# Two MLPs, attention between them: when weights are split, and in which order the seam to the last MLP runs

## The chip, the cores and the metric

The kernel runs on one core of a Trainium2 chip. The core has five engines with their own instruction queues: TensorE (PE, matrix products into PSUM), VectorE (DVE), ScalarE (ACT), GpSimd (POOL) and SyncE (SP, which here only issues DMAs). They meet only in semaphores: an engine adds to one when an instruction ends, another waits for a value. The metric is the device time of one launch in microseconds (us). The kernel before takes 1842.34 us, the median of three runs (1841.61 to 1843.49).

## The reference

Two layers on 1024 tokens (4 sequences of 256) of width 512, each stage ending in a normalized residual. What matters here:

```python
# layer 0: a state-space mixer (projection, convolution, scan, output projection), then an MLP on int weights
h = silu(x @ gate_w.T * gate_s) * (x @ up_w.T * up_s)     # 1376 hidden columns, padded to 11 tiles of 128
y = (h @ down_w.T) * down_s
# layer 1: attention, 32 query heads in 8 groups, rotary embedding, causal softmax, output projection Wo
# then an MLP whose weights are made from pairs (w, base):
d = w - base; weight = base + mean(abs(d)) * sign(d)      # w1, w3: 1792 hidden columns (14 tiles); w2: down
h = silu(x @ w1.T) * (x @ w3.T); out = h @ w2.T
```

Everything is float32. Matrix products are made in a faster form (fp32r) on pairs of operands: each operand is split into a high part (a rounded copy) and a low part (operand minus high part), and a product is the sum of high x high, high x low and low x high.

## The kernel before

The program is a row of phases, each a block in which every engine has its own list of instructions; at the end of a phase the engines meet at a barrier. In order: load, `n0` (first normalization), `in` (projection), `par`, `scan`, `fa` (output projection), `mi` (first MLP's widening), `fb` (first MLP's down projection), `kv` (keys and values), the attention phase with the last MLP's widening inside it, and `fd` (last down projection, results stored). `fa`, `fb` and `fd` are one function, `finish_phase`.

**finish_phase** goes over 8 tiles of 128 tokens. For tile t ScalarE copies the hidden tile to its high part `hh` (L253), GpSimd subtracts to get the low part `hl` (L300), TensorE does 3K products of 128x512 (L235 to L237; K is 11 in `fb`, 14 in `fd`), and VectorE, GpSimd and ScalarE normalize and add. Before the first tile the down weights themselves are split: ScalarE copies K rows to `wh` (L284), VectorE subtracts K rows to `wl` (L426), and TensorE's first tile waits for row k of both, and for `hh` and `hl`.

**widen_phase** (`mi`) goes over 11 tiles f of the hidden width: ScalarE makes the high part of weights f+1 (L523), VectorE the low part (L591), TensorE does 48 products (L503), ScalarE applies silu (L552), VectorE multiplies (L618). Beside it, in the first 8 steps, GpSimd subtracts (L579) and ScalarE sums absolutes (L528) of the last MLP's weight pairs, to find their mean difference. At its end SP loads the first MLP's down weights (`ahead`).

**The attention phase** goes over 8 groups g and 4 batches b. At batch b TensorE does the queries of the next batch (L1355), the output projection of the batch before (L1380 to L1382), the transposes and value products of this batch (L1389 to L1402), and the scores of the next one (L1366, L1368). The queries of the next batch are rotated before their scores: ScalarE turns them, GpSimd multiplies by the sine (L1631), VectorE by the cosine (L1703), and VectorE adds the two (`rotate`, L1710), which raises `q_done`. At b = 2 of groups 0 to 6, GpSimd subtracts the low part of the next group's query weights right behind the sine (`query_weights`, L1635), 2048 columns. At b = 0 it does the same for output weights (L1639).

**The seam** to the last MLP starts in the last group. Normalizations of attention's result (`y_moments_of`, `y_scale`, `y_shift`, `y_norm`), the residual (`residual`, GpSimd, L1647), normalizations for the MLP (`x_moments_of`, `x_scale`, `x_shift`, `x_norm`), transposes of tokens (L1412), their split (`token_high` L1530, `token_low` L1771), and the making of the first two weight tiles (`difference` GpSimd L1655, `difference_sign` ScalarE L1534, `whole` and `whole_down` VectorE L1778 and L1787, `mlp_high` ScalarE L1541, `mlp_low` GpSimd L1659) stand in each engine's list in an order written by hand. TensorE does hidden tiles 0 and 1 by halves of the tokens (`widen_batch`, parts of 24 products at L1418) as tokens come ready, and from tile 2 whole tiles of 48 products of 128x512. SP loads the next weight pair when both the low parts and the down row of two tiles before are made.

Of the kernel before, what the change touches and what calls it, by code (L numbers as in the profile page):

```python
# [159 lines left out]
def finish_phase(nc, tag, M, place, K, hidden=None, gate=None, w_raw=None, acc=None,  # L160
                 out_scale=None, last_out=None, norm_only=False, ahead=(), x_loads=()):
# [9 lines left out]
    gated, h_hi, h_lo = sem("hidden_gated"), sem("hidden_hi"), sem("hidden_lo")  # L171
    y_ready, scaled = sem("y_ready"), sem("y_scaled")
# [7 lines left out]
    if proj:  # L180
        wh = place("wh", [P, K, DM], F32R)
        wl = place("wl", [P, K, DM], F32R)
# [19 lines left out]
    with nc.Block() as block:  # L202
# [15 lines left out]
        def _(pe):  # L218
# [7 lines left out]
            def step(t, s):  # L226
                if proj and t < TT:
# [3 lines left out]
                    for k in range(K):  # L231
# [3 lines left out]
                        nc.tensor.matmul(ps_y[s], hh[s][:, k, :], wh[:, k, :], start=(k == 0), stop=False)  # L235
                        nc.tensor.matmul(ps_y[s], hh[s][:, k, :], wl[:, k, :], start=False, stop=False)  # L236
                        mm = nc.tensor.matmul(ps_y[s], hl[s][:, k, :], wh[:, k, :], start=False, stop=(k == K - 1))  # L237
# [8 lines left out]
        def _(act):  # L246
# [34 lines left out]
            if proj:  # L281
                hidden_hi(0, 0)
                for k in range(K):
                    nc.scalar.activation(wh[:, k, :], w_raw[:, k, :], ACT.Copy).then_inc(split_w, 1)  # L284
# [4 lines left out]
        def _(pool):  # L289
# [39 lines left out]
        def _(dve):  # L329
# [93 lines left out]
            if proj:  # L423
                for k in range(K):
                    dve.wait_ge(split_w, k + 1)
                    nc.vector.tensor_tensor(wl[:, k, :], w_raw[:, k, :], f32(wh[:, k, :]), ALU.subtract).then_inc(split_wl, 1)  # L426
# [8 lines left out]
def widen_phase(nc, tag, M, place, F, kind, raw_dram, base_dram=None, hidden=None,  # L435
                x_conv=None, gate=None, scales=None, coeff=None, second=None, diff=None, raw=None, base=None, ahead=()):
# [12 lines left out]
    tap = sem("tap")  # L449
    d_in, d_sub, d_abs = [sem("diff_in0"), sem("diff_in1")], sem("diff_sub"), sem("diff_abs")  # L450
# [7 lines left out]
    if diff is not None:  # L458
        DC = DIFF_COLS // N_SUMS
        dw = [place(f"dw{i}", [P, 3, DC]) for i in range(2)]  # L460
        dm = [place(f"dm{i}", [P, 3, DC]) for i in range(2)]
# [6 lines left out]
    with nc.Block() as block:  # L468
# [43 lines left out]
        def _(act):  # L512
# [17 lines left out]

            def step(f, s):
                if exists(f + 1, F):
                    prepare(f + 1, 1 - s)
                if diff is not None and exists(f, N_SUMS):
                    differences(f, s)
                if kind == "ssm":
# [51 lines left out]
        def _(dve):  # L588
# [12 lines left out]
            def step(f, s):  # L601
                if kind == "int" and exists(f + 1, F):
                    int_lows(f + 1, 1 - s)
                if kind == "diff" and exists(f + 1, F):
# [20 lines left out]
            paired_steps(dve, F, step)  # L625
            if kind != "ssm":
                dve.wait_ge(second_done, F)
# [1451 lines left out]
```

## Time and profile before

| | |
|---|---|
| median of 3 runs | 1842.34 us (1841.61 to 1843.49) |
| the profiled execution: its time, its span | 1840.51 us, 1838.7 us |
| PE busy | 1676.4 us (91%) |
| PEld, DVE | 1376.5 us (75%), 1097.3 us (60%) |
| ACT, POOL | 869.0 us (47%), 822.2 us (45%) |
| mean granted clock of TensorE | 0.971 |

The profile is of one execution. Busy time is the time in which an engine ran an instruction; PEld is TensorE's weight load beside its products. Rows of the timeline give the start, the duration, the engine, the line and the operands of one or more instructions; in brackets the idle time before them and what ended it. The granted clock (PEclk) is a share of TensorE's full speed, 1.0 being 2.4 GHz and 0.5 being 1.2 GHz.

### The profile page before, as it was taken

To read this page: it belongs to the slowest core of one execution; us is meant where nothing else is said; L and a number is where in the kernel's file an instruction comes from. 1 tells how busy PE (TensorE), PEld (TensorE's weight loads), DVE (VectorE), ACT (ScalarE), POOL (GpSimd) and SP (SyncE) were. 2 spreads that over 40 slices of the span, in tenths; PEclk is the share of its full clock that TensorE was granted. 3 is DMA by queue.
4 is the path that set the end of the run, shared out by engine and by line. 5 is a ranking of instruction groups with operands and counts; after the bars stand their busy time and mean duration, and the time that the engine had idled before them with its cause. 6 is when DMAs were issued, how large, how long until landed. Compare 5 with 4: busy or idle time off the path is not lost. (4 is left out here: it accounts for less than half of the span.)

```text
span 1838.7 us, 24233 instructions
## 1 busy us (share of the span) xinstructions
PE 1676.4 (91%) x8214; PEld 1376.5 (75%) x8214; DVE 1097.3 (60%) x1592; ACT 869.0 (47%) x1761; POOL 822.2 (45%) x416
## 2 busy tenths in 40 slices
PE   5994999999998799898989999999999998799988
PEld 4851788888886688676877778787788786778777
DVE  4326999999995332452915666666666767622232
ACT  2336777777763353333624445454444545433231
POOL 2200999999984362342512232222222323365353
PEclk9997999999999899998999999999999999999989
DMA  3101100011100394001100010000100010144100
GB/s 113 63 1 72 47 35 35 36 34 35 34 0 24 134 355 163 18 1 57 63 23 24 24 47 23 23 23 23 46 23 23 23 58 35 70 142 160 42 18 29
DMA packets 25188, 100.84 MB, mean 55 GB/s; under 512 B 3104, under 2 KB 3360, under 8 KB 22560
## 3 DMA queue, kind: packets, MB, share of 16 engines
q1 hardware_dynamic: 24976, 99.89, 15.1%
q8 instruction: 40, 0.66, 0.1%
q14 instruction: 28, 0.23, 0.0%
q10 hardware_dynamic: 144, 0.07, 0.0%
HBM read 97.72 MB, written 2.23 MB: 54 GB/s over the span
## 5 line engine op out<-in xcount | busy, mean ns | idle before, releaser
L1001 PE MATMUL psum<-scratch_s,res_const 128*128 128x256 f32 x1024 | 250.4, 383 | 4.7 <-DVE scratch_s L960 4.0
L1631 POOL TENSOR_TENSOR stretch_turned<-stretch_turned,res_const 128x1024 f32<-128x1024 f32 x32 | 80.3, 2509 | 386.6 <-ACT stretch_turned L1492 386.6
L1001 PEld LDWEIGHTS psum<-scratch_s,res_const 128*128 128x128 f32 x1024 | 191.8, 190 | 43.0 <-DVE scratch_s L960 18.3
L858 POOL TENSOR_TENSOR scratch_s<-scratch_s,scan_cm 128x1024 f32<-128x1024 f32 x64 | 150.9, 2358 | 27.6 <-DVE scratch_s L944 27.6
L944 DVE TENSOR_TENSOR_SCAN scratch_s<-psum,scratch_s 128x512 f32<-128x512 f32 x128 | 153.4, 1198 | 8.5 <-ACT psum L899 8.5
L1355 PE MATMUL psum<-opnd_xh,query_wqh 128*128 128x256 f32 x512 | 151.5, 296 | 1.9 <-PEq L94 1.9
L846 POOL TENSOR_TENSOR scratch_s<-scan_bm,scratch_s 128x1024 f32<-128x1024 f32 x64 | 150.9, 2359 | 0.1
L1355 PE MATMUL psum<-opnd_xh,query_wql 128*128 128x256 f32 x512 | 145.6, 284 | 0.0
L1355 PE MATMUL psum<-opnd_xl,query_wqh 128*128 128x256 f32 x512 | 145.5, 284 | 0.0
L1500 ACT ACTIVATE stretch_pa<-psum,stretch_nm 128x128 f32<-128x128 f32 x128 | 45.2, 365 | 197.0 <-DVE stretch_nm L1722 197.0
L995 PE MATMUL psum<-scan_diag,scratch_s 128*128 128x256 f32 x512 | 132.9, 383 | 0.5 <-ACT scratch_s L891 0.5
L899 ACT ACTIVATE psum<-ssm_dt,ssm_vec 128x255 f32 (+1 forms) x256 | 110.8, 465 | 11.8 <-DVE scratch_s L944 11.3
L995 PEld LDWEIGHTS psum<-scan_diag,scratch_s 128*128 128x128 f32 x512 | 95.9, 193 | 13.0 <-ACT scratch_s L891 0.9
L1355 PEld LDWEIGHTS psum<-opnd_xh,query_wqh 128*128 128x128 f32 x512 | 99.0, 193 | 3.2 <-issue 2.3
L1380 PE MATMUL psum<-stretch_woh,stretch_oh 128*128 128x512 f32 x256 | 100.3, 392 | 0.5 <-DVE stretch_ol L1823 0.5
L1381 PE MATMUL psum<-stretch_wol,stretch_oh 128*128 128x512 f32 x256 | 100.0, 390 | 0.0
L1382 PE MATMUL psum<-stretch_woh,stretch_ol 128*128 128x512 f32 x256 | 99.9, 390 | 0.0
L1355 PEld LDWEIGHTS psum<-opnd_xl,query_wqh 128*128 128x128 f32 x512 | 98.9, 193 | 0.8
L1355 PEld LDWEIGHTS psum<-opnd_xh,query_wql 128*128 128x128 f32 x512 | 98.7, 193 | 0.0
L235 PE MATMUL psum<-stretch_wh,stretch_hh 128*128 128x512 f32 x176 | 71.1, 404 | 17.2 <-ACT stretch_wh L284 15.5
L960 DVE TENSOR_TENSOR scratch_s<-psum,scan_cm 128x512 f32<-128x512 f32 x128 | 85.2, 665 | 0.0
L950 DVE TENSOR_TENSOR_SCAN psum<-scan_decay,psum 128x512 f32<-128x512 f32 x64 | 78.1, 1221 | 0.0
(269 smaller groups left out, 4322.4 us busy)
## 6 DMA issues: line engine op xcount, KB each, us to landing
mi_dw<-in_dw SPq DMA_DIRECT2D x24, 448.0 KB, 5.7
mi_dm<-in_dm SPq DMA_DIRECT2D x24, 448.0 KB, 6.4
query_raw<-in_w_q SPq DMA_DIRECT2D x8, 1024.0 KB, 4.7
query_raw<-in_w_o SPq DMA_DIRECT2D x8, 1024.0 KB, 4.8
scan_cm<-bc_rows SPq DMA_DIRECT2D x12, 512.0 KB, 4.1
gu_raw<-in_w_gu SPq DMA_DIRECT2D x11, 512.0 KB, 8.0
mlpa_raw<-in_w_mlp SPq DMA_DIRECT2D x7, 768.0 KB, 4.3
mlpa_base<-in_b_mlp SPq DMA_DIRECT2D x7, 768.0 KB, 5.8
```

Source lines behind the costliest of these rows:

```text
L846: nc.gpsimd.tensor_tensor(by_state(shared[r][h]), bm[:, 4 * h:4 * h + 4, :], u[r].rearrange("p (a t) -> p a t", a=1).broadcast_to((P, 4, S ...
L858: nc.gpsimd.tensor_tensor(shared[r][h], shared[r][h], weights(4 * h, 4), ALU.mult).then_inc(weighted_pool, 1)
L899: ins = nc.scalar.activation(by_state(bank)[:, n, 1:SEQ], flat_dt[:, bass.ds(s * SEQ + 1, SEQ - 1)], ACT.Exp, scale=M.vec[:, bass.ds(s * N ...
L944: nc.vector.tensor_tensor_scan(quarter(r, i), decay_shared[i % 2], quarter(r, i), 0.0, ALU.mult, ALU.add).then_inc(scanned, 1)
L960: nc.vector.tensor_tensor(own[i], state[i], weights(NH + 2 * i, 2), ALU.mult).then_inc(weighted, 1)
L995: mm = nc.tensor.matmul(by_state(state[i])[:, :, t * P:(t + 1) * P], ut[r][:, t * P:(t + 1) * P], diag[:, t, 2 * i:2 * i + 2, :], start=Tr ...
L1001: mm = nc.tensor.matmul(ps_y[r], ident, part[:, n * SEQ:(n + 1) * SEQ], start=False, stop=stop and (n + 1) * SEQ == part.shape[1])
L1355: mm = nc.tensor.matmul(ps_q[:, h * SEQ:(h + 1) * SEQ], w[:, k, h * HD:(h + 1) * HD], x[:, k, b * SEQ:(b + 1) * SEQ], start=(k == 0 and w ...
L1380: nc.tensor.matmul(X[t], oh[:, t, part], woh[:, h, :], start=(h == 0), stop=False)
L1381: nc.tensor.matmul(X[t], oh[:, t, part], wol[:, h, :], start=False, stop=False)
L1382: mm = nc.tensor.matmul(X[t], ol[:, t, part], woh[:, h, :], start=False, stop=(h == HPG - 1))
L1631: nc.gpsimd.tensor_tensor(heads(turned[:, :]), heads(turned[:, :]), over_heads(C_SIN, SEQ), ALU.mult).then_inc(q_sine, 1)
```

## The change

1. `query_weights` on GpSimd (b = 2, groups 0 to 6) waits for `q_done` of the batch whose sine it has just made. In the last group `difference(1)` moves behind the same wait, `residual(0)`, `residual(1)` and `mlp_low(0)`.
2. The hand-written order of the seam changes on all four engines.
3. The down weights of the last MLP are split in its widening: ScalarE and VectorE do row f-1 at step f. Those of the first MLP are split in steps 7 to 10 of `mi`; they are loaded in phase `fa` now. Low parts are made in place.
4. `finish_phase` with ready halves (`fb`, `fd`) begins otherwise: `hh` of the first tile in two parts, TensorE does all products with `wh`, then with `wl`, then waits for `hl`, which VectorE makes, and not GpSimd.
5. Places of tiles in SBUF change to suit.

```diff
@@ finish_phase, TensorE
+                if proj and t == 0 and halves is not None:
+                    pe.wait_ge(h_first, 1)
+                    for k in range(K):
+                        if k == K // 2:
+                            pe.wait_ge(h_hi, 1)
+                        nc.tensor.matmul(ps_y[s], hh[s][:, k, :], wh[k], start=(k == 0), stop=False)
+                    for k in range(K):
+                        nc.tensor.matmul(ps_y[s], hh[s][:, k, :], wl[k], start=False, stop=False)
+                    pe.wait_ge(h_lo, 1)
+                    for k in range(K):
+                        mm = nc.tensor.matmul(ps_y[s], hl[s][:, k, :], wh[k], start=False, stop=(k == K - 1))
+                    mm.then_inc(y_ready, 1)
@@ finish_phase, ScalarE
+            if proj and halves is not None:
+                nc.scalar.activation(hh[0][:, 0:K // 2, :], hidden(0, 0)[:, 0:K // 2, :], ACT.Copy).then_inc(h_first, 1)
+                nc.scalar.activation(hh[0][:, K // 2:K, :], hidden(0, 0)[:, K // 2:K, :], ACT.Copy).then_inc(h_hi, 1)
@@ finish_phase, GpSimd
-                hidden_low(0, 0)
+                if halves is None:
+                    hidden_low(0, 0)
+                else:
+                    pool.wait_ge(h_lo, 1)
@@ finish_phase, VectorE
+            if proj and halves is not None:
+                dve.wait_ge(h_hi, 1)
+                nc.vector.tensor_tensor(hl[0][:, :, :], hidden(0, 0), f32(hh[0][:, :, :]), ALU.subtract).then_inc(h_lo, 1)
@@ widen_phase: rows_at = {f: range((f - 7) * F // 4, (f - 6) * F // 4) for f in range(7, F)}
+                for k in rows_at[f]:                       # ScalarE, before the silu of step f
+                    nc.scalar.activation(next_wh[:, k, :], next_raw[:, k, :], ACT.Copy).then_inc(next_hi, 1)
+                    for k in rows_at[f]:                   # VectorE, before the product of step f
+                        dve.wait_ge(next_hi, k + 1)
+                        nc.vector.tensor_tensor(next_wl[:, k, :], next_raw[:, k, :], f32(next_wh[:, k, :]), ALU.subtract).then_inc(next_lo, 1)
@@ attention phase, last MLP
+    def down_rows(f):
+        return {2: (0,), 3: (1,), 4: (2, 3), F1 - 1: (F1 - 2, F1 - 1)}.get(f, (f - 1,))
...
+                nc.scalar.activation(down_halves[0][k], down[:, k, :], ACT.Copy).then_inc(down_hi, 1)
...
+                nc.vector.tensor_tensor(down_halves[1][k], down[:, k, :], f32(down_halves[0][k]), ALU.subtract).then_inc(down_lo, 1)
@@ TensorE
             weights_split(0)
             pe.wait_ge(exped, U)
             widen_batch(0, 0)
+            token_transposes(2)
+            token_transposes(3)
             weights_split(1)
             widen_batch(1, 0)
-            token_transposes(2)
-            token_transposes(3)
-            widen_batch(0, 1)
             token_transposes(4)
             token_transposes(5)
+            widen_batch(0, 1)
             widen_batch(1, 1)
             pe.wait_ge(added, 2 * U)
             widen_batch(2, 2)
             token_transposes(6)
+            token_transposes(7)
             pe.wait_ge(half_kept, 1)
             widen_batch(3, 2)
-            token_transposes(7)
@@ GpSimd, body
                 if b == 2 and not (isinstance(g, int) and g == GROUPS - 1):
+                    pool.wait_ge(q_done, g * BATCH + b + 2)
                     query_weights(g + 1)
...
                 if ending(g, b, 2):
-                    difference(1)
+                    pool.wait_ge(q_done, U)
                     residual(0)
                     residual(1)
                     mlp_low(0)
+                    difference(1)
@@ VectorE, body and after it
                 if last:
+                    x_shift(0)
                     y_moments_of(1)
+                    whole(1)
+                    y_shift(1)
...
                 if ending(g, b, 2):
                     values(g, b + 1, v + 1)
+                    whole_down(0)
                     accumulate(v, b)
-                    x_moments_of(0)
                 if more(g, b):
                     probabilities(*after(g, b))
                 if ending(g, b, 2):
-                    x_shift(0)
+                    x_moments_of(0)
...
+            whole_down(1)
+            x_shift(1)
             accumulate(U - 1, BATCH - 1)
...
-            whole_down(0)
-            whole_down(1)
...
```

## Rows read from the trace of the kernel before

**Rows 1.** TensorE's waits: line, releaser: us in total, times, longest.

```profile
PE psum L1366 <- DVE stretch_q L1710: 21.9, 9, 5.9
PE psum L235 <- ACT stretch_wh L284: 15.5, 2, 9.0
...
PE psum L1389 <- DVE stretch_pb L1733: 7.7, 2, 4.5
PE psum L1418 <- issue: 4.6, 1, 4.6
...
PE psum L1412 <- ACT norm_xn L1525: 1.7, 1, 1.7
```

**Rows 2.** TensorE's groups by line: busy us, mean ns, idle before and releasers.

```profile
L1418 PE MATMUL psum<-opnd_xh,mlpa_wh 128*128 128x512 f32 (+1 forms) x128 | 46.8, 366 | 6.2 <-DVE opnd_xl L1771 3.0 <-DVE hidden_hidden L1794 1.9 <-POOL mlpa_wl L1659 1.3
```

**Rows 3.** Timeline at batch 2 of group 1: GpSimd, VectorE, TensorE.

```profile
1091.97 4.55 POOL L1635 TENSOR_TENSOR query_wql<-query_raw,query_wqh 128x2048 fp32r<-128x2048 f32 x1
...
1091.71 0.69 DVE L1739 TENSOR_TENSOR acc_acc<-psum,acc_acc 128x512 f32<-128x512 f32 x1 [0.23 <-PE psum L1382]
...
1093.19 4.41 DVE L1710 TENSOR_TENSOR stretch_q<-stretch_direct,stretch_turned 128x1024 f32<-128x1024 f32 x1
...
1097.75 1.15 PE L1366 MATMUL psum<-att_k,stretch_q 128*128 x8 [2.06 <-DVE stretch_q L1710]
...
1100.28 0.47 PE L1355 MATMUL psum<-opnd_xh,query_wqh 128*128 128x256 f32 x1
```

**Rows 4.** All 32 rotations: duration in ns, least, median, most.

```profile
L1710 DVE TENSOR_TENSOR stretch_q<-stretch_direct,stretch_turned x32: 1214/1217/4414, 963.4 to 1542.2; 128x1024 f32<-128x1024 f32 x32
```

**Rows 5.** Timeline at the start of `fb`.

```profile
751.83 1.38 ACT L253 ACTIVATE fb_hh<-mlp_hidden 128x1408 fp32r<-128x1408 f32 x1 [6.62 <-PEq L94]
...
753.28 3.16 POOL L300 TENSOR_TENSOR fb_hl<-mlp_hidden,fb_hh 128x1408 fp32r<-128x1408 f32 x1 [48.78 <-ACT fb_hh L253]
753.76 9.26 DVE L426 TENSOR_TENSOR fb_wl<-mlp_down,fb_wh 128x512 fp32r<-128x512 int32 x11 [2.94 <-ACT fb_wh L284]
...
757.14 0.77 PE L235 MATMUL psum<-fb_wh,fb_hh 128*128 128x512 f32 x1 [7.64 <-DVE fb_wl L426]
```

**Rows 6.** Timeline at the start of `fd`.

```profile
1747.08 1.70 ACT L253 ACTIVATE stretch_hh<-hidden_hidden 128x1792 fp32r<-128x1792 f32 x1 [6.93 <-PEq L94]
1748.85 3.98 POOL L300 TENSOR_TENSOR stretch_hl<-hidden_hidden,stretch_hh 128x1792 fp32r<-128x1792 f32 x1 [19.94 <-ACT stretch_hh L253]
1749.33 11.89 DVE L426 TENSOR_TENSOR stretch_wl<-down_down,stretch_wh 128x512 fp32r<-128x512 f32 x14 [3.54 <-ACT stretch_wh L284]
...
1753.54 0.77 PE L235 MATMUL psum<-stretch_wh,stretch_hh 128*128 128x512 f32 x1 [9.01 <-ACT stretch_wh L284]
```

**Rows 7.** Busy us (count) by stretch: PE, PEld, DVE, ACT, POOL; PEclk, DMA share, GB/s.

```profile
980.50:983.90 3.40, 3.40 (x8) 1.61 (x7) 2.23 (x3) 1.19 (x2) 0.96 (x1) 0.56 0.00 0
...
1754.00:1758.70 4.70, 4.70 (x13) 3.60 (x13) 4.70 (x8) 3.65 (x5) 0.98 (x1) 0.54 0.01 3
757.20:762.00 4.80, 4.80 (x12) 3.80 (x13) 4.80 (x9) 2.99 (x5) 1.73 (x1) 0.54 0.00 0
```

**Rows 8.** Timeline of the seam: VectorE, then GpSimd.

```profile
1555.60 1.28 DVE L1758 BATCH_NORM_STATS2 stretch_ln<-tok_x 128x6 f32<-128x512 f32 x2
...
1569.80 3.15 DVE L1778 SCALAR_TENSOR_TENSOR mlpb_raw<-mlpb_raw,res_coeff,mlpb_base 128x512 f32<-128x512 f32 x2
...
1594.65 3.27 DVE L1767 SCALAR_TENSOR_TENSOR stretch_ln<-stretch_ln 128x2 f32<-128x2 f32 x1
...
1594.41 3.49 POOL L1655 TENSOR_TENSOR mlpa_raw<-mlpa_raw,mlpa_base 128x1536 f32<-128x1536 f32 x1 [1.36 <-DMA mlpa_base<-in_b_mlp]
```

**Rows 9.** Timeline, step 5 of the last widening (GpSimd), step 8 of `mi` (ScalarE, VectorE).

```profile
1650.36 2.39 POOL L1659 TENSOR_TENSOR mlpa_wl<-mlpa_raw,mlpa_wh 128x1024 fp32r<-128x1024 f32 x1 [5.03 <-ACT mlpa_wh L1541]
...
722.34 1.12 ACT L552 ACTIVATE mi_mid<-psum,gu_gate_s 128x1024 f32<-128x1024 f32 x1 [4.32 <-PE psum L503]
...
727.91 1.28 DVE L618 SCALAR_TENSOR_TENSOR mlp_hidden<-psum,gu_up_s,mi_mid 128x1024 f32 x1 [8.38 <-PE psum L503]
```

More of the change, by code:

```diff
@@ L180, in finish_phase @@
     if proj:
-        wh = place("wh", [P, K, DM], F32R)
-        wl = place("wl", [P, K, DM], F32R)
+        if halves is None:
+            w_hi, w_lo = place("wh", [P, K, DM], F32R), place("wl", [P, K, DM], F32R)
+            wh, wl = [w_hi[:, k, :] for k in range(K)], [w_lo[:, k, :] for k in range(K)]
+        else:
+            wh, wl = halves
         hh = [place(f"hh{i}", [P, K, P], F32R) for i in range(2)]
@@ L321, in _ @@
                 gating(1, 1)
-                hidden_low(0, 0)
+                if halves is None:
+                    hidden_low(0, 0)
+                else:
+                    pool.wait_ge(h_lo, 1)
                 hidden_low(1, 1)
@@ L459, in widen_phase @@
         DC = DIFF_COLS // N_SUMS
-        dw = [place(f"dw{i}", [P, 3, DC]) for i in range(2)]
-        dm = [place(f"dm{i}", [P, 3, DC]) for i in range(2)]
+        at, held = place.at, F * DM * 4
+        dw = [place("dw0", [P, 3, DC])]
+        dm = [place("dm0", [P, 3, DC])]
+        next_wh = Places(nc, f"{tag}_next", at, at + held)("wh", [P, F, DM], F32R)
+        place.at = at + held
+        dw.append(place("dw1", [P, 3, DC]))
+        dm.append(place("dm1", [P, 3, DC]))
+        next_raw, next_wl = next_w
+        M.next_halves = [next_wh[:, k, :] for k in range(F)], [next_wl[:, k, :] for k in range(F)]
+        M.next_range = at, at + held
+        rows_at = {f: range((f - 7) * F // 4, (f - 6) * F // 4) for f in range(7, F)}
         tail = F - N_SUMS + 1
@@ L535, in step @@
                     differences(f, s)
+                if diff is not None and isinstance(f, int) and f >= 7:
+                    next_highs(f)
                 if kind == "ssm":
@@ L624, in _ @@
                 int_lows(0, 0)
-            paired_steps(dve, F, step)
+            paired_steps(dve, F, step, tail=tail)
             if kind != "ssm":
                 dve.wait_ge(second_done, F)
+            if diff is not None:
+                dve.wait_ge(next_lo, F)
     signals.close()
@@ L1580, in body @@
                     nc.scalar.activation(oh[:, t, :], x, ACT.Copy).then_inc(o_hi, 1)
+                    if ending(g, b, BATCH - 1) and t == 0:
+                        y_norm(2)
                 if b == 0:
@@ L1623, in _ @@
                     mlp_high(f + 1)
+                for k in down_rows(f):
+                    down_high(k)
                 gate(f)
@@ L1681, in _ @@
             y_scale(1)
-            y_scale(2)
             residual(2)
             residual(3)
+            y_scale(2)
+            mlp_low(1)
             x_scale(1)
@@ L1687, in _ @@
             residual(5)
-            mlp_low(1)
+            y_scale(3)
             x_scale(2)
-            y_scale(3)
             residual(6)
@@ L1845, in _ @@
             groups(dve, body)
-            y_shift(1)
             y_moments_of(2)
@@ L1880, in _ @@
                     whole_down(f + 1)
+                for k in down_rows(f):
+                    down_low(k)
                 keep(f)
             dve.wait_ge(kept, F1 - 2)
+            dve.wait_ge(down_lo, F1)
     signals.close()
```

89 lines of the change are left out of this document (55 added, 34 removed).

## The prediction

> **What bounds the kernel now.** First the busy shares: TensorE is busy for 1676.4 of 1838.7 us, so a gain has to come from its idle time or its clock. The waits of TensorE [rows 1, 2] name the idle stretches that this change touches. Nine waits for a rotated query (L1710) make 21.9 us; the longest, 5.9, is the phase's first, the rest is eight of about 2.0. Two first products of a down projection wait 15.5 us in all for its split weights (the 9.0 is `fd`'s, the other `fa`'s, which keeps the old start), and `fb`'s waits 7.6 [rows 5]. The rest are the seam's: 4.5 for probabilities (of 7.7, the other 3.2 being early in the phase), 4.6 before the second weight tile, 1.7 for a normalized token tile, and 6.2 for low parts of tokens, a kept half and a weight tile. Then I read timelines at each of these places, and the granted clock behind them.
>
> Why the rotation is late is seen in [rows 3, 4]. The addition takes 1214 ns as a rule and up to 4414 at most. In the timeline it begins at 1093.19 while GpSimd's subtraction runs (1091.97 to 1096.52), and ends at 1097.60, which is 1.1 us after GpSimd's end: it stood still until then. An addition with one operand in PSUM (L1739) took its ordinary 0.69 beside the same subtraction. So two operands in SBUF are what collides. The same is seen at both down projections [rows 5, 6]: the first VectorE subtraction begins behind GpSimd's `hl` and finishes after it, and TensorE begins about 0.7 us after GpSimd's end.
>
> **GpSimd waits for the rotation (7 places).** The rotation ends at 1093.19 + 1.21 = 1094.40. TensorE is free at 1097.75 - 2.06 = 1095.69, so its scores begin then and end 2.53 later (1097.75 to 1100.28), at 1098.22. The next instruction on TensorE is the first query product of the next group, and it needs GpSimd's low part: 1094.40 + 0.1 + 4.52 (the subtraction's 4.55 less its overlap) + 0.1 = 1099.12. This is a new wait of 0.9, and the gain is 1100.28 - 1099.12 = 1.15 us, not the 2.06 of the wait removed. Queued behind GpSimd's new wait is only the subtraction and, 14 us later, the next sine; SP's load of output weights, which waits for the subtraction, comes 2.5 us later, with over 10 us before its use. In group 0 the old wait was about 0.3 shorter. Sum: 6 x 1.15 + 0.85 = 7.7 us. Bounds: 2.1 each if the subtraction were early enough (14.5), and 0 if GpSimd's start is 1.1 later than I say.
>
> **Start of `fb`.** ScalarE starts `hh` at 751.83 [rows 5], after the barrier, which stays. Now TensorE waits only for the first part, 5 of 11 tiles of 128 columns: by 1.38 for 1408 columns and 1.70 for 1792 [rows 5, 6] a column costs 0.83 ns and the start 0.2, so the first 640 columns take 0.7. First product at 751.83 + 0.70 + 0.12 = 752.65 instead of 757.14: 4.5 us. What is late next: the second part (at 753.3, wanted after five products, not before 753.8), then `hl` on VectorE, 1408 columns at 1.21 us per 1024 [rows 4], done at about 755.0 and wanted after 22 products, not before 757. So neither shows. The splitting of weights is gone from here. The later tiles of `fb` keep their rhythm.
>
> **Start of `fd`.** In the same way 896 columns take 0.93: 1747.08 + 0.93 + 0.12 = 1748.13 instead of 1753.54 [rows 6]: 5.4 us. `hl` on VectorE, 1792 columns, ends at about 1751.0 and is wanted after 28 products, 6.4 us after the start. GpSimd's low part of tile 1 runs next, 4.0 us, to 1755, wanted after 1757.6.
>
> **The clock behind these starts.** The products after both starts run at 0.54 of the clock for 4.7 and 4.8 us [rows 7], that is nearly all at 1.2 GHz: 2.4 us lost each. The new gaps are 3.2 and 3.6 us long. The nearest row is behind the 3.2 us wait early in the phase [rows 1]: there the clock is at 0.56 for 3.4 us [rows 7], lost 1.6. I take that: 0.8 gained at each place, 1.6 together. Bounds: 0 (as long as now) and 4.8 (no fall).
>
> **Where the splitting goes.** In `mi`, steps 7 to 10: up to 3 copies on ScalarE (0.53 each: 1.70 for 1792 columns comes to about as much for 512) and 3 subtractions on VectorE (0.6 to 0.84 each, 9.26 for 11 with the stall in it [rows 5]). ScalarE there sits idle 4.3 us before the silu, VectorE 8.4 before its product [rows 9], so 1.6 and 2.5 us lie in idle time; GpSimd's last subtraction in `mi` is over by then. Cost 0. Without that cover it would be 11 x 0.6 = 6.6 us. The down weights' load, 2816 KB, moves to `fa`, in front of no other load there, and is awaited at the end of a phase that moves 1 GB/s for 60 us: 0. In the last MLP each step gets one copy (0.6) and one subtraction (0.67). VectorE's will stand behind GpSimd's `mlp_low`, which begins just before it (1650.36, 2.39 us [rows 9]), and then hold up GpSimd's `difference` for 0.6. The low parts made at 1652.7 are wanted by TensorE some 4.5 us later. Cost 0, at most 10 x 0.67 if that margin were gone.
>
> On this collision the Trainium skill (SBUF — State Buffer, on its two sides) states that VectorE and GpSimd lock a shared port pair exclusively, whoever comes first and for the whole instruction. The trace agrees: 4.41 against 1.21. By the same rule GpSimd's larger instructions could win the lock in the seam more often now; what that would cost stands among the rivals, from rows.
>
> **The seam.** I walked the new lists of the four engines through from 1540, with the durations of the rows, and with two-operand instructions of VectorE held until GpSimd's end. In the old order the walk gave TensorE's waits within half a microsecond, but for one. The pieces:
> - The last rotation no longer stands behind `difference(1)`: 2.0.
> - Probabilities go ahead of the moments of x, which took 1.28 + 0.4 before them [rows 8]: 1.1 of the 4.5 wait; 3.4 stay.
> - `whole(1)` and `y_shift(1)` now precede the low parts of the last attention output on VectorE, and `y_shift(1)` needs GpSimd's `y_scale(1)`. The last output projection, which waited 0.5, waits 1.3 to 3.0: a loss of 0.8 to 2.5.
> - `whole(1)` is made near 1560 and not at 1569.80 (where GpSimd's residuals stretched it to 3.15 [rows 8]), so the 4.6 wait for the second weight tile goes. Transposes of tokens 2 and 3 now wait 2.2 for their normalization: a gain of 2.4.
> - The later waits were 1.7 + 6.2 = 7.9 [rows 1, 2]. The 1.7 came from `x_shift(3)`, a tiny instruction that took 3.27 because `difference(2)` ran from 1594.41 [rows 8]. In the new order the data of `difference(2)` will have landed long before, as `whole_down(0)` releases the load early, so GpSimd starts it right behind `x_scale(3)` and the same stall is certain; but TensorE then has three parts of 2.9 us each to do. The walk leaves 3.0 in all: a gain of 4.9.
> - Two stretches at 1.2 GHz (behind the 4.5 and the 4.6 waits) cost about 4.1; one is left: a gain of 2.4.
>
> Sum: 2.0 + 1.1 - 1.6 + 2.4 + 4.9 + 2.4 = 11.2 us. Bounds: 5 and 15.
>
> **The sum.** 7.7 + 4.5 + 5.4 + 1.6 + 11.2 = 30.4 us. The profiled execution took 1840.51 (span 1838.7, 1.8 around it), so 1810.1; the median of the runs lies 1.8 above that execution: 1811.9, say 1812.
>
> **Rivals.**
> A. The new stalls bite (chance 0.17): GpSimd's instructions win over VectorE's small ones at the seam, and the group's new wait for the low part takes what the rotation gave back. For it: 3.27 for a tiny instruction [rows 8], and the 0.9 wait that I already count. Against it: TensorE has whole parts queued at most of these places. Seam 5, groups 3: 30.4 - 6.2 - 4.7 = 19.5, that is 1823.
> B. More than I count (0.18): the clock stays up behind the shorter gaps (3.2 more), and the seam reaches 15: 37 us, 1805. For it: gaps of 2.06 in the groups mostly leave the clock up; against it: the 3.2 us gap with 0.56.
> C. The change of place does nothing at the down projections (0.02): something else than the split holds TensorE, such as the barrier. ScalarE starts at 751.83 and 1747.08 whatever follows. Then 9.9 + 1.6 are lost: 1823.5.
> D. Slower (0.03): the added VectorE subtractions in the last MLP hold GpSimd's port, and the low parts come too late in each step. It decides once they are delayed by more than the 4.5 us margin; at 10 steps it needs 7.5 us of delay each to eat 30 us, with 0.67 of added work. At 8 us each: 1812 + 10 x 3.5 = 1847.
>
> My forecast has 0.60. The range that holds 8 in 10 runs from 1804 to 1823. About 0.2% (3.7 us) is what a measurement can tell from no change. Faster by more than that: 0.95 (all but D and a remnant); within it 0.02; slower 0.03.
>
> **What would show it.** Rotations at batch 2 take 1.21 and none over 2 us; GpSimd's subtraction of query weights starts at their end; TensorE's first query product of a group waits about 0.9 for GpSimd. First products of `fb` and `fd` come 0.8 and 1.05 us after ScalarE's first instruction. No row of weight splitting in `fb` and `fd`. TensorE's idle time from the last rotation to the third weight tile falls from 19.4 (1.9 + 4.5 + 0.5 + 4.6 + 7.9) to about 10 us. TensorE has no wait in `mi` or in the last widening beyond tile 2. I am wrong if the wait for query weights is over 2 us, or if `fb` and `fd` begin later than 1.5 us after ScalarE's start.

## The result, and the profile after

The changed kernel takes 1811.12 us (median of four runs, 1809.98 to 1811.91) against 1842.16 us (1841.61 to 1843.49) for the kernel before in the same comparison: a ratio of 0.983, with a 95% interval of 0.9813 to 0.9847. It is faster by about 31 us. The forecast was 1812 with 1804 to 1823. The profiled execution took 1811.37 us, with a span of 1809.6. One execution of the changed kernel in e9's comparison (2877.04 us) and one of the kernel before beside it (2490.49) ran at a mean granted clock of 0.56 and 0.65; the ratios leave them out, and without them the medians given below for that comparison would be at most 0.3 us lower.

TensorE's waits in the changed kernel (line, releaser: us in total, times, longest) answer to [rows 1, 2]:

```profile
PE psum L1441 <- DVE stretch_pb L1798: 7.8, 2, 4.6
PE psum L236 <- ACT stretch_hh L298: 6.7, 2, 3.6
...
PE psum L1407 <- POOL query_wql L1698: 6.3, 6, 1.0
PE psum L1418 <- DVE stretch_q L1775: 5.9, 1, 5.9
...
PE psum L1464 <- ACT norm_xn L1577: 3.7, 3, 1.8
...
PE psum L1470 <- POOL mlpa_wl L1722: 0.9, 1, 0.9
PE psum L1432 <- DVE stretch_ol L1895: 0.8, 1, 0.8
```

Of 21.9 us for rotated queries 5.9 remain, the phase's first wait. In its place six waits for GpSimd's low part have come, 6.3 us in all, and a seventh, in group 0, of 0.7. The two starts of down projections now wait for the first part of `hh` (L298, 3.1 and 3.6 us of idle time), and not for weights. The 4.6 before the second weight tile is gone, the 4.6 for probabilities has stayed.

All 32 rotations in the changed kernel, as in [rows 4] (least, median and most in ns), and the timeline at batch 2 of group 1, as in [rows 3]:

```profile
L1775 DVE TENSOR_TENSOR stretch_q<-stretch_direct,stretch_turned x32: 1214/1215/1224, 960.0 to 1529.1; 128x1024 f32<-128x1024 f32 x32
```

```profile
1088.01 1.22 DVE L1775 TENSOR_TENSOR stretch_q<-stretch_direct,stretch_turned 128x1024 f32<-128x1024 f32 x1
...
1089.30 4.52 POOL L1698 TENSOR_TENSOR query_wql<-query_raw,query_wqh 128x2048 fp32r<-128x2048 f32 x1 [2.46 <-DVE stretch_q L1775]
...
1091.23 1.89 PE L1420 MATMUL psum<-att_k,stretch_q 128*128 x8
...
1094.17 0.35 PE L1407 MATMUL psum<-opnd_xh,query_wqh 128*128 128x256 f32 x1 [1.05 <-POOL query_wql L1698]
```

GpSimd starts 0.07 us after the rotation's end and ends at 1093.82; TensorE begins 0.35 later, having waited 1.05. The scores before it have no wait.

The starts of `fb` and of `fd`, as in [rows 5, 6]:

```profile
753.57 0.74 ACT L298 ACTIVATE stretch_hh<-mlp_hidden 128x640 fp32r<-128x640 f32 x1 [6.63 <-PEq L94]
...
754.36 2.08 PE L236 MATMUL psum<-mi_next_wh,stretch_hh 128*128 128x512 f32 x4 [3.14 <-ACT stretch_hh L298]
...
755.07 1.62 DVE L447 TENSOR_TENSOR stretch_hl<-mlp_hidden,stretch_hh 128x1408 fp32r<-128x1408 f32 x1 [2.53 <-ACT stretch_hh L299]
...
1723.01 0.95 ACT L298 ACTIVATE stretch_hh<-hidden_hidden 128x896 fp32r<-128x896 f32 x1 [6.95 <-PEq L94]
...
1724.01 2.50 PE L236 MATMUL psum<-down_high_wh,stretch_hh 128*128 128x512 f32 x5 [3.57 <-ACT stretch_hh L298]
```

The first product comes 0.79 and 1.00 us after ScalarE's start; the gap is 3.14 instead of 7.64, and 3.57 instead of 9.01. The clock there did not gain (busy us by stretch, and the clock behind them, columns as in [rows 7]):

```profile
754.36:760.80 6.44, 6.44 (x16) 5.10 (x17) 1.62 (x1) 1.95 (x2) 3.19 (x1) 0.54 0.38 123
1724.00:1730.20 6.20, 6.19 (x16) 4.89 (x17) 2.02 (x1) 2.39 (x2) 3.27 (x1) 0.55 0.01 3
```

These are 6.4 and 6.2 us near 1.2 GHz, longer than the 4.8 and 4.7 of before [rows 7].

**Where the time came from.** Marks on TensorE in both traces, and what each stretch between two marks gained (positive is faster):

| mark | before | after | gained since the mark above |
|---|---|---|---|
| first product of `mi` | 627.41 | 628.92 | -1.5 |
| first product of `fb` | 757.14 | 754.36 | 4.3 |
| first product of `kv` | 837.39 | 835.22 | -0.6 |
| first scores of attention | 964.67 | 961.24 | 1.3 |
| first query product of group 1 (made at batch 2 of group 0) | 1025.64 | 1020.56 | 1.65 |
| the same product, made in group 6 | 1474.72 | 1461.83 | 7.8 |
| third weight tile, second half | 1619.11 | 1595.07 | 11.15 |
| first product of `fd` | 1753.54 | 1724.01 | 5.5 |
| last product's end | 1832.22 | 1803.06 | -0.4 |

The sum is 29.2, and the span fell by 29.1. The -1.5 lies in phases that the change does not touch: at 122 the clock of the changed kernel's execution is down for 3.4 us, that of before not. In another execution of the changed kernel (e9 below) the first product of `mi` comes at 627.41, as before.

The 1.65 has two parts. TensorE's wait in group 0 fell from 1.77 to 0.72 us, about 1.0 in all. The other 0.7 was gained before the first place that the change touches. Attention's first scores come in a low stretch. In the kernel before (columns as in [rows 7]):

```profile
964.70:969.80 5.10, 5.10 (x17) 4.47 (x17) 0.00 (x0) 0.00 (x0) 0.00 (x0) 0.50 0.01 3
```

after:

```profile
961.30:964.90 3.60, 3.60 (x13) 3.24 (x14) 0.00 (x0) 0.00 (x0) 0.00 (x0) 0.50 0.02 5
```

The first lasts 5.1 us at half speed, the second 3.6. In the same way the 7.8 is six times 1.03, and 1.6 from a low stretch of the kernel before at 1321.8, shown under e1.

### The profile page after: what moved, and what is told of

Its sections match the earlier page's. It is cut to its first block and busy times, and to the rows that moved or that the text cites. A ratio compares the mean times of both kernels' runs of the same rounds, so it can differ in the third digit from the quotient of the medians.

```text
span 1809.6 us, 24213 instructions
## 1 busy us (share of the span) xinstructions
PE 1674.1 (93%) x8214; PEld 1374.3 (76%) x8214; DVE 1097.2 (61%) x1594; ACT 868.9 (48%) x1763; POOL 811.4 (45%) x414
## 5 line engine op out<-in xcount | busy, mean ns | idle before, releaser
L948 ACT ACTIVATE psum<-ssm_dt,ssm_vec 128x255 f32 (+1 forms) x256 | 110.8, 465 | 11.7 <-DVE scratch_s L993 11.2
L999 DVE TENSOR_TENSOR_SCAN psum<-scratch_s,psum 128x512 f32<-128x512 f32 x64 | 78.0, 1219 | 0.0
```

Of the source, the lines that this page charges most:

```text
L948: ins = nc.scalar.activation(by_state(bank)[:, n, 1:SEQ], flat_dt[:, bass.ds(s * SEQ + 1, SEQ - 1)], ACT.Exp, scale=M.vec[:, bass.ds(s * N ...
L999: nc.vector.tensor_tensor_scan(state[i], decay_own[i % 2], state[i], 0.0, ALU.mult, ALU.add).then_inc(scanned, 1)
```

## Experiments

Each is timed against the kernel before on the same chip; gains are differences of medians. "After" is the changed kernel. The kernel before took 1842.16 in the main comparison, 1841.97 in that of e1 to e4, 1840.25 in that of e5 to e8 and 1841.58 in that of e9 to e11, so two versions from different comparisons can be set against each other to about 2 us. After's own gain was 31.0 us, and 32.2 when it was run again as e9.

**Does the sum divide as forecast?** Three kernels do one part each.

e1, the wait alone, on the kernel before:

```diff
                 if b == 2 and not (isinstance(g, int) and g == GROUPS - 1):
+                    pool.wait_ge(q_done, g * BATCH + b + 2)
                     query_weights(g + 1)
```

> The kernel before with one line more: GpSimd waits for the rotated query before it subtracts the low part of the next group's query weights (groups 0 to 6). Theory A (two-operand instructions of VectorE stand still until GpSimd's ends; TensorE then waits 1.05 us for GpSimd instead of 2.06 for the rotation): all rotations but the last take 1.2 us, each of seven groups gains 1.0 us, and the 1.7 us lost to the low clock after one of the old waits goes too: 1842.2 - 7.1 - 1.7 = 1833.4 us, between 1832.5 and 1836. Rival B (the gain seen in the groups of the changed kernel comes from elsewhere, and the subtraction made later costs as much as the rotation gives): 1842 us, with TensorE waiting 2 us for GpSimd.

Measured: 1832.45 us (1830.17 to 1833.22) against 1841.97, ratio 0.995 (0.9933 to 0.9966), a gain of 9.5, about 1 more than the 8.8 expected. Its trace has the same six waits as after, and its clock is at 1.00 from 1316 to 1330, where before has a stretch at 1.2 GHz:

```profile
PE psum L1355 <- POOL query_wql L1635: 6.4, 6, 1.1
```

```profile
1316.00:1330.00 14.00, 12.94 (x83) 11.48 (x81) 7.59 (x18) 5.37 (x18) 4.33 (x2) 1.00 0.21 75
```

The same columns in the kernel before:

```profile
1321.80:1325.20 3.40, 3.40 (x14) 3.08 (x14) 0.71 (x2) 0.00 (x0) 0.00 (x0) 0.55 0.64 265
```

e2, the splitting and the new start of down projections alone, is the changed kernel with the wait and the seam taken back:

```diff
-                    pool.wait_ge(q_done, g * BATCH + b + 2)
                     query_weights(g + 1)
...
@@ the seam on all four engines: the order of the kernel before
```

> The changed kernel with GpSimd's wait taken out and the old order of the seam on all four engines: only the splitting of the down weights during widening and the new start of the two down projections are left. Theory A (the parts add up): starts gain 4.5 + 5.4, the clock gives 0.8 back, the rest stands as before: 1842.2 - 9.1 = 1833 us, between 1831.5 and 1834.5. Rival B (the added subtractions on VectorE cost something in the widening or in the seam, which the new order hides): 1836 to 1839 us, with waits of TensorE in either widening that the kernel before does not have.

Measured: 1834.13 us (1831.83 to 1834.9), ratio 0.9953 (0.9937 to 0.997), a gain of 7.8. The forecast's terms for this part are 9.9, and 11.5 with the clock; 9.1 was expected when the clock at the starts was known. The trace shows what is missing. e2 keeps the old wait, and three of its seven old waits are followed by a low stretch, where before has one:

```profile
1096.60:1099.90 3.30, 3.30 (x10) 2.61 (x9) 0.01 (x1) 0.00 (x0) 0.00 (x0) 0.50 0.49 204
1171.70:1175.00 3.30, 3.30 (x12) 3.03 (x13) 0.97 (x2) 0.00 (x0) 0.00 (x0) 0.50 0.72 290
1472.10:1475.40 3.30, 3.30 (x12) 2.85 (x11) 0.48 (x1) 0.00 (x0) 0.00 (x0) 0.50 0.67 276
```

Two more of 3.4 us at half speed cost 3.4 us. e2's span is 5.6 below that of the kernel before, and would be 9.0 below it without them. Rival B, a cost of the splitting, is not needed.

e3, the seam alone, is the kernel before with the four new lists, the wait for the last rotation in them; groups 0 to 6 stay as they were:

```diff
@@ the seam on all four engines: the order of the changed kernel
                 if ending(g, b, 2):
-                    difference(1)
+                    pool.wait_ge(q_done, U)
                     residual(0)
                     residual(1)
                     mlp_low(0)
+                    difference(1)
...
```

> The kernel before with only the new order of the seam, the wait for the last rotation in it. Theory A (the parts add up): 11.2 us less, 1831 us, between 1829 and 1833. Rival B (the new order pays only because the groups before it run faster or because the down weights are split beside it): 1835 us or more.

Measured: 1830.5 us (1829.45 to 1831.65), ratio 0.994 (0.9923 to 0.9956), a gain of 11.5. The three gains sum to 28.8, the whole gave 31.0 and 32.2 in other comparisons; the interval of each is about 3 us wide to either side, so the parts are independent as far as this can tell.

The old wait of 1.8 to 2.1 us occurs seven times in groups 0 to 6 of each kernel that has it. In the three traces (before, e2, e3) a stretch of about 3.4 us at 1.2 GHz follows it in 5 of 21 places: 1, 3 and 1. In the seven traces with the new wait of 0.7 to 1.1 us it follows in none of 49.

**What in the new start does it?** e4 is after, with the first tile's products of `fb` and `fd` in the old order, waiting for all of `hh` and `hl`:

```diff
                     pe.wait_ge(h_first, 1)
-                    for k in range(K):
-                        if k == K // 2:
-                            pe.wait_ge(h_hi, 1)
-                        nc.tensor.matmul(ps_y[s], hh[s][:, k, :], wh[k], start=(k == 0), stop=False)
...
+                    pe.wait_ge(h_hi, 1)
+                    pe.wait_ge(h_lo, 1)
+                    for k in range(K):
+                        nc.tensor.matmul(ps_y[s], hh[s][:, k, :], wh[k], start=(k == 0), stop=False)
+                        nc.tensor.matmul(ps_y[s], hh[s][:, k, :], wl[k], start=False, stop=False)
+                        mm = nc.tensor.matmul(ps_y[s], hl[s][:, k, :], wh[k], start=False, stop=(k == K - 1))
```

> The changed kernel, but the first tile of the first MLP's and of the last down projection does its three products of a row together, as all other tiles do, and so waits at its start for both halves of the hidden tile and for its low part. Theory A (the order of the products is a part of the gain, as VectorE's low part is ready only 2.9 us after today's start in the last projection and 2.4 in the first MLP's): 1811.1 + 5.3 = 1816.4 us, up to 2 less if the clock is warmer when the products run, which it should not be: 1814.5 to 1817.5. Rival B (taking the weight splitting away is all of the gain, and the start does not matter since a later tile's wait sets the pace): 1811 us.

Measured: 1816.03 us (1815.37 to 1818.5), 4.9 above after (by gains 5.1), ratio 0.9861 (0.9845 to 0.9878). TensorE's waits of e4 say where it went:

```profile
PE psum L236 <- DVE stretch_hl L444: 12.2, 2, 6.6
```

Two waits of 12.2 stand where after has two of 6.7: 5.5 us. So of the 9.9 gained at both starts 5.5 come from starting on what is ready, which is the order of the products together with `hh` in two parts, and 4.4 from splitting the weights early. The two were not told apart further.

**Can the new wait in the groups go too?** e5 is after, with the subtraction of query weights in two parts of 1024 columns, one behind the sine and one behind the rotation:

```diff
+                nc.gpsimd.tensor_tensor(flat(wql)[:, 0:WQ], raw[:, 0:WQ], f32(flat(wqh))[:, 0:WQ], ALU.subtract)
...
+                    query_weights(g + 1)
                     pool.wait_ge(q_done, g * BATCH + b + 2)
-                    query_weights(g + 1)
+                    query_weights_rest(g + 1)
```

> The changed kernel, with GpSimd's subtraction of query weights in two instructions of 1024 columns: the first right behind the sine, the second behind the wait for the rotation. Theory A (VectorE's two-operand instruction stands still until GpSimd's current one ends, no longer, and takes its turn before the next): the rotation begins under the first part and takes 2.2 us, still in time for its scores; the second part ends before TensorE wants the weights; TensorE's waits for GpSimd (6 of 1.05, one of 0.72) go: 1811.1 - 7.0 = 1804.1 us, 1803 to 1805.5. Rival B (GpSimd's second part is queued at once and keeps VectorE out until both are done, or the start of a second instruction costs what it saves): rotations of 4 us again and 1811 us or more.

Measured: 1802.71 us (1801.68 to 1802.74) against 1840.25, ratio 0.9795 (0.978 to 0.981), 8.4 below after's 1811.12, and 6.7 below after's 1809.38 of another comparison. By gains it is 37.5, which is 6.5 and 5.3 more than after's. Expected was 7.0, with 5.6 to 8.1 as its range; the four differences span it. The rotation and GpSimd's parts in e5:

```profile
L1780 DVE TENSOR_TENSOR stretch_q<-stretch_direct,stretch_turned x32: 1212/1215/2243, 959.0 to 1520.5; 128x1024 f32<-128x1024 f32 x32
```

```profile
1084.93 2.35 POOL L1699 TENSOR_TENSOR query_wql<-query_raw,query_wqh 128x1024 fp32r<-128x1024 f32 x1
1088.45 2.36 POOL L1702 TENSOR_TENSOR query_wql<-query_raw,query_wqh 128x1024 fp32r<-128x1024 f32 x1 [1.16 <-DVE stretch_q L1780]
```

The rotation is held up by 1.0 us at most and TensorE still has work then: its transposes and value products run without a gap from 1084.8 to 1088.5, when the scores begin. Its list of waits has no `query_wql` left. The 6.3 us of six waits and 0.7 of the first are gone, as expected.

**Does the clock follow from the gaps?** e6 is after with products that nobody reads: five at the end of each widening, and four before the first tile of `fb` and `fd`.

```diff
+                for _ in range(5):
+                    nc.tensor.matmul(ps[1][0][:, 0:HALF], wh[0][:, 0, 0, :], M.xh[:, 0, 0:HALF], start=True, stop=True)
...
+                    for _ in range(4):
+                        nc.tensor.matmul(ps_t[0], wh[0][:, 0:P], wh[0], start=True, stop=True)
                     pe.wait_ge(h_first, 1)
```

> The changed kernel with products that nobody reads: 5 of 128x512 behind the last product of each widening and 4 at the start of the down projections of both MLPs, so that TensorE's idle time before those starts falls from 3.1 and 3.6 us to about 1.5. Theory A (the low clock over the first 6.4 and 6.2 us of these projections is owed to the idle time before them): it stays high, 1811.1 - 3.2 - 3.1 = 1804.8 us, 1803.5 to 1807. Rival B (the low clock comes at the barrier whatever TensorE does shortly before): clock as before and 1811 to 1812 us.

Measured: 1807.97 us (1807.76 to 1808.31), ratio 0.9823 (0.9808 to 0.9838), 3.2 below after where 6.3 were expected, and by gains only 1.2. It was repeated beside after on one chip, as e10 and e9:

> The kernel with unread products around the two starts, once more, beside the changed kernel on one chip: the first comparison gave 1.3 us of the 6.3 expected, across two chips. Theory A (the clock stays up at both starts, but the next low stretch, at the end of the first MLP's projection, ends at the same moment as before, so that half of what the first start gains is lost again; a low stretch of 3.4 us in the seam came by chance): 1.3 + 2.5 = 3.8 us below the changed kernel, or 2.1 where the seam's stretch comes again. Rival B (the unread products are in the way, and cost what the clock gives): no difference.

> The changed kernel once more, on the chip of the two below, as their base: 0.983 of the kernel before, as the first time. No theory differs on it.

Measured: e9 1809.38 us, ratio 0.9828 (0.9815 to 0.9841); e10 1806.93 us (1805.94 to 1809.07), ratio 0.9816 (0.9803 to 0.9829). The difference is 2.45, between the two values expected for theory A. The products do what they should: from 754.0 on the clock in e6 is at 1.00. What happens behind it is seen at the start of `kv`, in e6:

```profile
754.00:760.40 6.40, 6.40 (x29) 5.27 (x29) 1.63 (x1) 2.48 (x3) 3.22 (x1) 1.00 0.40 124
...
835.20:838.60 3.40, 3.40 (x10) 2.66 (x9) 0.00 (x0) 0.00 (x0) 0.00 (x0) 0.50 0.45 140
...
838.60:839.40 0.80, 0.80 (x5) 0.62 (x4) 0.00 (x0) 0.00 (x0) 0.00 (x0) 0.84 0.00 0
839.50:842.50 3.00, 3.00 (x14) 2.45 (x14) 0.05 (x1) 1.11 (x2) 0.00 (x0) 1.00 0.00 0
```

and in after:

```profile
835.20:838.60 3.40, 3.38 (x8) 2.72 (x9) 0.00 (x0) 0.00 (x0) 2.34 (x2) 0.50 0.51 151
838.60:839.40 0.80, 0.80 (x4) 0.62 (x4) 0.00 (x0) 0.00 (x0) 0.00 (x0) 0.91 0.68 177
839.50:842.50 3.00, 3.00 (x15) 2.47 (x14) 0.00 (x0) 0.00 (x0) 0.00 (x0) 1.00 0.10 37
```

e6's first product of `kv` starts at 832.76, after's at 835.22, and in both the clock is back at full speed near 839. The 2.5 us that e6 is ahead are spent at 1.2 GHz, where half of them is lost: its first scores start at 960.00, only 1.2 ahead of after's 961.24. There the same happens again:

```profile
960.00:965.10 5.10, 5.10 (x17) 4.47 (x17) 0.00 (x0) 0.00 (x0) 0.00 (x0) 0.50 0.01 3
```

The full clock is back at 965.2, after's at 965.0, and from 974.4 on e6 is only 0.6 ahead. So of what is gained at `fb` half is given back one phase later and another 0.7 at the start of attention. At `fd` e6 begins its useful products 0.5 ahead and ends 3.1 ahead. Added up: 2.7 gained at `fb`, 2.6 at `fd`, 2.0 given back, and 0.2 that e6 was behind when `mi` began. That is the 3.1 by which the two profiled executions differ, and it is why 6.3 was too much.

e9 and e10 settle rival B, that unread products are in the way. e10 is 1.3 behind e9 at the first scores, because it began `mi` 1.1 later, is 1.2 behind at the first useful product of `fd` (1722.74 and 1721.50), and ends 1.6 ahead (1799.20 and 1800.80). It gains 2.8 at `fd` alone, nothing at `fb`.

e9 showed something that neither theory had. It is the changed kernel unchanged, but its `fb`, behind the same gap of 3.14 us, runs at full clock:

```profile
752.60:759.00 6.40, 6.37 (x28) 5.25 (x29) 1.62 (x1) 1.98 (x2) 3.21 (x1) 1.00 0.36 124
1721.50:1728.00 6.50, 6.50 (x16) 5.11 (x17) 2.03 (x1) 2.37 (x2) 3.58 (x1) 0.53 0.01 3
```

So there was nothing left for unread products to gain at `fb` in e10. And e9, which has none, gives back as e6 does: it is 4.4 ahead of after at the first product of `kv` (830.81) and 3.3 ahead at the first scores (957.94).

And behind the same 3.57 or 3.58 us at `fd` the low stretch was 6.2 us or more in after and e9, but only 3.4 in e5 (e7 has 3.4 as well):

```profile
1715.60:1719.00 3.40, 3.40 (x9) 2.73 (x10) 2.03 (x1) 2.33 (x2) 0.52 (x1) 0.58 0.02 5
1719.00:1722.50 3.50, 3.50 (x17) 2.87 (x17) 0.00 (x0) 0.00 (x0) 3.50 (x1) 1.00 0.00 0
```

The length of a gap of this size does not fix what it costs. The Trainium skill (TensorE: Matmul & The Clock Gate, Part 1) states that how many products run slow at the start of a kernel varies between runs of one kernel. Here the same is seen behind a gap inside the kernel, with 0 and 6.4 us at `fb` in two executions.

**The stall in the seam.** e7 is after, with GpSimd waiting for `x_shift(3)` before `difference(2)`:

```diff
             x_scale(3)
+            pool.wait_ge(x_shifted, TT // 2)
             for f in range(2, F1):
                 difference(f)
```

> The changed kernel, with GpSimd waiting for the last x_shift before its subtraction for the third weight tile. Theory A (x_shift takes 3.46 us only because that subtraction has begun): x_shift takes 0.15 us, the tokens 6 and 7 come 3.3 us earlier, and TensorE's 0.66 wait before their transposes goes; the subtraction comes 0.3 us later, which the wait for the third weight tile (0.89) passes on in part: 1811.1 - 0.4 = 1810.7 us. Rival B: the late tokens are covered entirely by the three parts queued on TensorE, and only the weights' delay shows: 1811.4 us. The two are closer than the runs can tell; the traces decide.

Measured: 1808.89 us (1808.12 to 1811.06), ratio 0.9833 (0.9818 to 0.9848). VectorE and GpSimd in after:

```profile
1574.39 3.46 DVE L1832 SCALAR_TENSOR_TENSOR stretch_ln<-stretch_ln 128x2 f32<-128x2 f32 x1 [0.81 <-POOL stretch_ln L1714]
...
1574.32 3.51 POOL L1718 TENSOR_TENSOR mlpa_raw<-mlpa_raw,mlpa_base 128x1536 f32<-128x1536 f32 x1
```

and in e7:

```profile
1573.29 0.16 DVE L1833 SCALAR_TENSOR_TENSOR stretch_ln<-stretch_ln 128x2 f32<-128x2 f32 x1 [0.81 <-POOL stretch_ln L1714]
...
1573.53 3.52 POOL L1718 TENSOR_TENSOR mlpa_raw<-mlpa_raw,mlpa_base 128x1536 f32<-128x1536 f32 x1 [0.28 <-DVE stretch_ln L1833]
```

An instruction on two columns takes 0.16 in place of 3.46, and TensorE's wait of 0.66 behind it is gone. On the total this can't be told from nothing: 2.2 and 0.5 below the two medians of after, and by gains 0.3 more and 0.8 less than theirs.

**Together.** e8 is e5, e6 and e7 in one. e11 adds unread products on either side of the last transposes of `fa` and `fb`:

```diff
                 if not store and t >= lag:
+                    if proj and t >= TT:
+                        unread(9)
                     transposes(t - lag, (t - lag) % 2)
+                    if proj and t == TT + lag - 1:
+                        unread(8)
```

> The changed kernel with all three: subtraction in two parts, unread products around the starts, x_shift before the third tile's subtraction. Theory A (each acts at its own place): 1811.1 - 7.0 - 6.3 - 0.4 = 1797.4 us, 1796 to 1800. Rival B (neither of the first two does what I say): 1811 us; one alone about 1804.5.

Measured: 1798.94 us (1797.34 to 1799.61), ratio 0.9771 (0.9757 to 0.9784). The time lies in the expected range, but partly because the kernel before was fast in this comparison: the gain over after's is 10.3 or 9.1 us where 13.7 were added up. Beside e5 on the same chip it is 3.8 lower where 6.7 were added up; the missing 2.9 are those of e6, since `kv` and attention begin as in e6.

> The kernel with all three edits and, on top, unread products in TensorE's idle time at the ends of the scan's output projection and of the first MLP's (9 before each of the last two transposes, 8 behind them). Theory A (the low stretches of 13.7 us there are owed to this idle time; they cover the first 5.7 us of the first MLP's widening and the first 4.2 us of the keys' and values' phase): 7.0 (two parts) + 3.8 + 2.8 + 2.1 + 1.0 for the transposes = 16.7 us below the changed kernel, 14 to 18. Rival B (the unread products stand in front of the transposes and delay them, or the stretches stay): 9 to 11 us below it, as the kernel with the three edits.

Measured: 1794.49 us (1792.98 to 1794.97), ratio 0.9746 (0.9733 to 0.9759), 14.9 below after on the same chip, where 14 to 18 was expected. It is 4.5 below e8, and by gains 5.8. The stretch at the start of `mi` in e8, and in e11:

```profile
620.90:634.60 13.70, 6.74 (x19) 5.21 (x20) 4.97 (x9) 3.90 (x5) 0.55 (x1) 0.53 0.52 190
```

```profile
620.90:634.60 13.70, 8.90 (x41) 6.82 (x40) 4.86 (x8) 3.90 (x5) 0.55 (x1) 1.00 0.53 189
835.20:838.60 3.40, 3.40 (x16) 2.82 (x15) 1.23 (x1) 1.54 (x2) 1.09 (x1) 1.00 0.03 10
```

Both phases that follow these normalizations, `mi` and `kv`, now start at full clock. e11 is the fastest version of all, 47 us below the kernel before.

## Why the prediction was right, and where it was not

- **GpSimd waits for the rotation: 7.7 forecast, 7.2 measured, and 9.5 with what the clock did.** The mechanism held: all rotations take 1.21 to 1.22, and the new wait is 1.05 where 0.9 was forecast, so a group gains 1.03 and not 1.15. Group 0 gained 1.0, forecast 0.85. The marks show 1.65 + 7.8 = 9.45; of this 0.7 is the low stretch at attention's start, which ended sooner after the first scores, and 1.6 the low stretch at 1321.8 that went with the old wait. The forecast had neither term. e1's 9.5 holds the second too.
- **Start of `fb` and `fd`: 4.5 and 5.4 forecast, 4.5 and 5.4 measured** (7.64 - 3.14; 9.01 - 3.57). The offsets of the first product from ScalarE's start, 0.82 and 1.05, came out at 0.79 and 1.00. Rival C is refuted: ScalarE starts where the barrier lets it, and the products follow the split.
- **The clock behind these starts: 1.6 forecast, about -1.0 measured.** This is the term that was mis-sized. By the marks the stretches behind `fb` and `fd` lost 0.6 and 0.4. The 0.56 for 3.4 us behind a 3.2 us gap [rows 1, 7] was taken as the price of a gap of that length. e9 and e5 show that there is no such price: 0 to 6.4 us at 1.2 GHz behind the same gap. The bounds, 0 to 4.8, excluded a loss, and that was the error in them: nothing in the rows excluded a longer low stretch behind a shorter gap. Rival B, the clock stays up, is what e9 had at `fb`; which of the two came in the profiled execution was chance.
- **Splitting hidden: 0 forecast, 0 measured.** TensorE is busy without a gap from 629 to 751, after the wait of 4.7 at the start of `mi` that the kernel before has too. A copy there takes 0.62, not 0.53 (the recorded fit, 0.2 + 0.83 ns a column, gives 0.62 as well), which changes nothing. In the last widening each added subtraction takes 2.47, as it stands behind `mlp_low`, and holds GpSimd's `difference`, 3.95 in the median where 3.50 was the duration before. TensorE is busy without a gap from 1600 to 1720. The rows of after:

```profile
L1857 DVE TENSOR_TENSOR down_low_wl<-down_down,down_high_wh x10: 2467/2474/3981, 1597.5 to 1681.2; 128x512 fp32r<-128x512 f32 x10
```

```profile
L1718 POOL TENSOR_TENSOR mlpa_raw<-mlpa_raw,mlpa_base x7: 3513/3952/3963, 1502.3 to 1683.1; 128x1536 f32<-128x1536 f32 x7
```

```profile
1600.00:1720.00 120.00, 120.00 (x531) 99.38 (x530) 63.73 (x55) 43.04 (x44) 62.58 (x20) 1.00 0.33 119
```

  Rival D falls with this: GpSimd's delay is 0.45 per step, and TensorE waits for nothing.
- **The seam: 11.2 forecast, 11.15 measured** (e3 alone 11.5). The waits left are 4.56, 0.81, 1.84, 1.15, 0.66 and 0.89, which is 9.9; about 10 was forecast, out of 19.4. So the waits gave 9.5 where 8.8 was forecast, and the clock 1.7 where 2.4 was. The pieces are less good than the sum: the wait for probabilities did not shrink (4.56 against 4.5), where 1.1 was to be gained; the last output projection waits 0.81, below the 1.3 to 3.0 that was feared. The stall of `x_shift(3)` is there as foreseen, and costs TensorE 0.66 (e7). "One low stretch is left" was right for this execution; e9, e6 and e10 have a second one of 3.4 us near 1560 to 1566. It costs nothing: e9's waits in the seam are 8.5 and not 9.9, and e9 is 2.5 ahead of after on both sides of it (e6 0.6 and 0.5).
- **Rival A**, the new stalls bite, did not come: the new wait stayed within 0.2 of what was counted, and the stall in the seam costs 0.66.
- The forecast total was 30.4, the profiled executions differ by 29.1 and the medians by 31.0. It met the number this closely by luck too, because errors of both signs cancel: -0.5 in the groups' waits, +1.6 from the low stretch at 1321.8, +0.7 at attention's start, +1.3 ahead of attention, where the low stretch of `kv` ends at 839 and not at 844, against -2.6 in the clock at the starts and -1.5 from a clock stretch in untouched phases.

What stays open: why the low stretch at `fb` is 6.4 us in one execution of the changed kernel and absent in another, and why 5 of 21 waits of 2 us were followed by one. No run sets the clock by itself. The traces are one execution of each version, so the shares of luck are known for these executions and not for the medians.

## What to carry to other kernels

When VectorE's operation with two SBUF operands takes several times its ordinary duration, look at what GpSimd runs then; order GpSimd's long work behind it, or cut the work so that the piece ahead fits into the slack. A projection whose operands are split needs only the first part of the high halves to begin: order its products by what is ready first, and split its weights where the engines were idle. Estimate gaps and instruction times from rows, but give every term that hangs on the clock a range that goes below zero, and, where a later phase starts at low clock, expect what was won before it to come out smaller (e6 lost 1.2 of 2.5 at `kv`) or larger (the changed kernel gained 1.3 there).

## What the runs showed of the hardware

- The same gap of TensorE gave different stretches at 1.2 GHz: 3.14 us gave 6.4 us in one execution and none in another; 3.57 us gave 6.5, 6.2 and 3.4 us.
- In attention's groups a gap of TensorE of 1.8 to 2.1 us was followed by about 3.4 us at 1.2 GHz in 5 of 21 places, a gap of 0.7 to 1.1 us in none of 49.
- The start of a phase and the return of the full clock did not move together. `kv`'s products began at 837.4, 835.2 and 832.8 (before, after, e6), and the full clock came at 844, 839 and 839. Attention's scores began at 964.7, 961.2 and 960.0, and it came at 970, 965 and 965.
- A low stretch among waits can cost nothing: with 3.4 us more of it in the seam, e9's waits there were 1.4 shorter.
- GpSimd and VectorE hold each other both ways: a two-column instruction of VectorE took 3.46 us beside GpSimd's subtraction of 3.51, and GpSimd's subtraction took 3.95 instead of 3.50 beside a subtraction of VectorE that takes 0.69 alone. An evenly cut GpSimd subtraction cost little: 2.35 and 2.36 us for two halves of one that takes 4.52.
- In `fa` and `fb` 26 more unread products each raised the mean granted clock of the profiled executions from 0.974 to 0.983 and took 4.5 us off the median (5.8 by gains; e8 to e11), though TensorE did more work.
